# Attention's output projection of a batch: in one group through the pair banks, or in eight one-bank pieces through the score ring, over six groups

## The reference, cut to what matters

```
q, k = rope(x @ Wq.T + bq), rope(x @ Wk.T + bk)        # 16 heads, two maps (1, 2) of 16 columns each
s1, s2 = q1 @ k1.T / 4, q2 @ k2.T / 4                  # 1024 x 1024, causal
attn = softmax(s1) - lam * softmax(s2)
out = attn @ v                                         # per head 1024 x 16
out = out * rsqrt(mean(out * out, -1) + eps) * head_norm_w * (1 - li)
x = layernorm(x + out.reshape(B, S, 256) @ Wo.T + bo)
```

## Time and profile before

| | us |
|---|---|
| median of 3 runs | 2443.26 |
| lowest, highest | 2440.05, 2448.67 |
| the profiled execution | 2444.31 |
| its span (first to last instruction) | 2442.5 |
| mean granted TensorE clock in it | 0.966 of full |
| PE busy in the span | 2217.5 (91%) |
| DVE, ACT, POOL busy | 1581.1, 1244.2, 713.6 |
| the 32 groups, between ACT's copies at step 6 of groups 1 and 31 | 1358.14 to 2220.72 |

### The profile page before, as it was taken

One profiled execution on the slowest core, in us unless ns is written; L12 is line 12 of the kernel. 1 busy time (PEld: TensorE's weight loads), 2 busy tenths in 40 slices (PEclk: granted clock), 3 DMA queues, 4 the chain that ended last, 5 costly groups with the idle time before them and its releaser, 6 DMA issues.

```text
span 2442.5 us, 50583 instructions
## 1 busy us (share of the span) xinstructions
PE 2217.5 (91%) x17816; PEld 1367.4 (56%) x17816; DVE 1581.1 (65%) x2653; ACT 1244.2 (51%) x2537; POOL 713.6 (29%) x797
## 2 busy tenths in 40 slices
PE   7999999889999999976866999899989998999998
PEld 5777777556666666655652333333333334347887
DVE  3556666643333333338999888788878887844878
ACT  6666665213433322323322778777767876774110
POOL 1222322102333333325553232422232342223000
PEclk9999999999999999988885999999999999999999
DMA  4223334651222222232431011010001100210000
GB/s 170 87 87 103 114 113 164 207 200 32 53 36 38 38 36 38 38 98 97 164 141 41 28 48 39 30 43 33 32 25 52 37 28 28 63 37 1 18 26 27
DMA packets 89900, 164.19 MB, mean 67 GB/s; under 512 B 15952, under 2 KB 64080, under 8 KB 88000
## 3 DMA queue, kind: packets, MB, share of 16 engines
q1 hardware_dynamic: 76032, 142.20, 16.9%
q0 software_dynamic: 13632, 18.77, 4.8%
HBM read 99.91 MB, written 60.49 MB: 66 GB/s over the span
## 4 chain that ended last, share of the span: by engine, by line
PE 54%; DVE 11%; ACT 6%; issue 5%; DMA 2%; SPq 0%; POOL 0%; ACTq 0%; DVEq 0%
PE PS L2169 10%; PE PS L1404 8%; PE PS L58 6%; PE PS L60 6%; PE PS L59 6%; PE PS L2232 6%; PE PS L2193 4%; ACT E L1983 4%; DVE NM L2079 3%; PE PS L2188 2%; PE PS L1389 2%; DVE X L2416 2%; DVE TT L1597 2%; PE PS L2123 1%; PE PS L2144 1%
## 5 line engine op out<-in xcount | busy, mean ns | idle before, releaser
L2079 DVE TENSOR_REDUCE NM<-PS 128x2 f32<-128x1024 f32 (+3 forms) x608 | 679.9, 1160 | 138.2 <-PE PS L2193 131.9
L1983 ACT ACTIVATE E<-PS 128x512 f32<-128x512 f32 (+2 forms) x1280 | 626.1, 560 | 206.7 <-PE PS L2232 194.9
L2169 PE MATMUL PS<-E,VP 128*32 128x256 f32 (+1 forms) x5120 | 370.8, 371 | 0.5 <-ACT OT L2010 0.5
L1916 POOL TENSOR_SCALAR_AFFINE_SELECT E<-E 128x512 f32<-128x512 f32 x256 | 162.5, 635 | 411.7 <-ACT E L1983 411.6
L1201 DVE SCALAR_TENSOR_TENSOR XIL<-PS,XSC,XIH 128x128 f16<-128x128 f32 x142 | 43.2, 346 | 335.4 <-ACT XIH L997 335.4
L2232 PE MATMUL PS<-QK 50*128 50x512 f16 (+3 forms) x1152 | 214.2, 329 | 16.2 <-ACT E L1983 16.0
L1032 ACT ACTIVATE HB<-PS 128x768 f32<-128x768 f32 x71 | 57.6, 811 | 300.8 <-PE PS L1389 300.8
L2169 PEld LDWEIGHTS PS<-E,VP 128*32 128x32 f32 x5120 | 108.4, 109 | 161.0 <-issue 117.3
L1404 PE MATMUL PS<-WALL,HB 128*128 x852 | 195.7, 379 | 1.0 <-ACT HB L1032 1.0
L2193 PE MATMUL PS<-QK 48*128 48x512 f16 (+3 forms) x1152 | 180.6, 344 | 9.6 <-DVE NM L2079 9.0
L941 POOL DMA_INDIRECT XB<-x_normed,IDX x71 | 71.1, 1001 | 364.9 <-DVE GAT L1217 315.5
(11 more groups left out here) (347 smaller groups left out, 4178.6 us busy)
## 6 DMA issues: line engine op xcount, KB each, us to landing
parts<-PP SPq DMA_DIRECT2D x32, 512.0 KB, 3.0
WIN<-in_we SPq DMA_DIRECT2D x16, 768.0 KB, 5.2
QK<-parts SPq DMA_DIRECT2D x96, 128.0 KB
WALL<-pairs_of_weights SPq DMA_DIRECT2D x7, 1536.0 KB
pairs_of_weights<-WPH SPq DMA_DIRECT2D x16, 384.0 KB, 2.3
pairs_of_weights<-WPL SPq DMA_DIRECT2D x16, 384.0 KB, 3.2
WALL<-in_we SPq DMA_DIRECT2D x8, 768.0 KB
QK<-parts SPq DMA_DIRECT2D x96, 64.0 KB
```

The costliest lines, as they stand in the source:

```text
L1916: e.affine_select(out=E[:, m % NE, :, 0:128], in_=E[:, m % NE, :, 0:128], pattern=[[0, 4], [1, 128]], compare_op=ALU.is_ge, fill=0.0, base ...
L1983: e.activation(dst, src, ACT.Exp, scale=unit).then_inc(S.ex, 1)
L2079: e.tensor_reduce(dst, src, AX, ALU.max).then_inc(S.mx, 1)
L2169: a = e.matmul(PS[32 * jj:32 * jj + 32, 7, 512 - n + c0:512 - n + c1], VP[b % 2][:, kt, 17 * hd:17 * hd + 32], E[:, m % NE, jj, c0:c1], st ...
```

## The change

The loops over steps are replaced by one generator `steps()`, which yields for every step the letters of a table (s scores, v products, m maximum, x select, and so on), and after the last letter of a step the mark "end". It leaves scores, products and maxima in the order of before. On POOL, one mask of E (step 5) goes ahead of the two small copies of the row maxima, in each group. The end of a batch is then laid out anew by tables with keys (group of the batch, step):

- DVE's sum of squares is four instructions of 512 values, at the ends of steps 16, 18, 20, 22 of group 8b + 8 (`meant`).
- POOL scales one eighth a step in steps 2 to 9 of group 8b + 9 (`scaled`).
- the transposes are four pieces of four (`joined`), at the ends of steps 12 and 18 of groups 8b + 9 and 8b + 10, each into one bank and copied out by one ACT instruction of 128x512.
- the product with Wo is four pieces of four matmuls (`put_out`), at the end of step 12 of groups 8b + 11 to 8b + 14, each into one bank; DVE adds 128x512 at the end of step 13 (`added`) and takes two moments; roots at step 15 (`rooted`) and norms at 17 and 19 (`normed`) of groups 8b + 12 and 8b + 14.
- these eight pieces take their turns in the ring of the three score banks (`single`), and no longer in the pair banks. The score tile that comes third after a piece takes the bank of that piece: it waits for ACT's copy (`S.pj`) or DVE's add (`S.op`) in place of an exponential.

The diff, cut:

```diff
+    STEPS = (
+        "msvm", "svxm", "svm", "sxO", "srRm", "svxhLm", "svH", "svxm", "svm", "svm", "svm", "sodm", "sAm",
...
+    halves = [(0, 0), (0, 1), (1, 0), (1, 1), (2, 0), (3, 0)] + [(4 + k // 2, k % 2) for k in range(12)] + [(10, 0), (11, 0)]
+    OVER = 3
...
+    joined = {(1, 12): 0, (1, 18): 1, (2, 12): 2, (2, 18): 3}
+    put_out = {(3, 12): 0, (4, 12): 1, (5, 12): 2, (6, 12): 3}
+    added = {(3, 13): 0, (4, 13): 1, (5, 13): 2, (6, 13): 3}
+    rooted = {(4, 15): 0, (6, 15): 1}
+    normed = {(4, 17): 0, (4, 19): 1, (6, 17): 2, (6, 19): 3}
+    squared = {(0, 13 + i): i for i in range(8)}
+    scaled = {(1, 2 + i): i for i in range(8)}
+    all_squared = (0, 23)
+    meant = {(0, 16): 0, (0, 18): 1, (0, 20): 2, (0, 22): 3}
...
+    def single(key, sem, value):
+        bank = singles[len(single_turns) % 3]
+        single_turns[key] = (bank, single_freed.get(bank))
+        single_freed[bank] = (sem, value)
...
+        if c == "s" and w >= 0:
+            for i in scores_of(w, s):
+                single(("score", i), S.ex, i + 1)
+        if c == "end":
+            if k in joined:
+                single(("join", b, joined[k]), S.pj, 4 * b + joined[k] + 1)
+            if k in put_out:
+                single(("out", b, put_out[k]), S.op, 4 * b + put_out[k] + 1)
...
+        def join_part(b, j):
+            kb, _ = single_turns["join", b, j]
+            c = slice(512 * (j // 2), 512 * (j // 2) + 512)
+            e.wait_ge(S.pe_pj, 4 * b + j + 1)
+            e.wait_ge(S.ms, 4 * b + 4)
+            e.activation(OTT[:, j % 2, c], PS[:, kb, :], ACT.Copy).then_inc(S.pj, 1)
...
-    def norm_x(e, b, q):
-        xs = [X[:, 8 * b + 4 * q + i, :] for i in range(4)]
-        e.wait_ge(S.rs4, 2 * b + q + 1)
-        layernorm_apply(e, K, xs, xs)[-1].then_inc(S.xd, 1)
...
+        def means_of(b, c):
+            e.wait_ge(S.sq1, 8 * b + 2 * c + 2)
+            e.tensor_reduce(MS[:, 32 * c:32 * c + 32], OB[:, 2 * c:2 * c + 2, :].rearrange("p i (h d) -> p (i h) d", d=16), AX, ALU.add).then_inc(S.ms, 1)
+
+        def add_out(b, q):
+            kb, _ = single_turns["out", b, q]
+            xs = X[:, 8 * b + 2 * q:8 * b + 2 * q + 2, :]
+            e.wait_ge(S.pe_op, 4 * b + q + 1)
+            e.wait_ge(S.bo, b + 1)
+            e.tensor_tensor(xs, xs, PS[:, kb, :].rearrange("p (i d) -> p i d", i=2), ALU.add).then_inc(S.op, 1)
+
+        def moments(b, q):
+            c, t0 = 2 * (q % 2), 8 * b + 2 * q
+            e.wait_ge(S.op, 4 * b + q + 1)
+            a = layernorm_stats(e, own.dve, K.ST[:, c:c + 2, :], K.MV[:, c:c + 2, :], [X[:, t0 + i, :] for i in HALF])
+            if q % 2:
+                a.then_inc(S.mv4, 1)
+
+        def norm_two(b, q):
+            e.wait_ge(S.rs4, 2 * b + q // 2 + 1)
+            for i in HALF:
+                x, c = X[:, 8 * b + 2 * q + i, :], 2 * (q % 2) + i
+                a = e.tensor_scalar(x, x, K.MV[:, c, 0:1], K.RS[:, c:c + 1], ALU.subtract, ALU.mult)
+            if q % 2:
+                a.then_inc(S.xd, 1)
...
+                if k in meant:
+                    means_of(b, meant[k])
+                if k in normed:
+                    norm_two(b, normed[k])
+                if k in added:
+                    add_out(b, added[k])
+                    moments(b, added[k])
...
+        def join_part(b, j):
+            kb, free = single_turns["join", b, j]
+            k, h = j % 2, j // 2
+            e.wait_ge(*free)
+            e.wait_ge(S.osc1, 8 * b + 4 * h + 4)
+            for i in QUAD:
+                a = e.transpose(PS[:, kb, 128 * i:128 * i + 128], OA[b % 2][:, 4 * h + i, 128 * k:128 * k + 128], K.IDN[:])
+            a.then_inc(S.pe_pj, 1)
+
+        def out_part(b, q):
+            kb, free = single_turns["out", b, q]
+            e.wait_ge(*free)
+            e.wait_ge(S.pj, 4 * b + 2 * (q // 2) + 2)
+            e.wait_ge(S.hnw, 2)
+            for i in HALF:
+                t = 2 * q + i
+                for k in HALF:
+                    a = e.matmul(PS[:, kb, 256 * i:256 * i + 256], OTT[:, k, 128 * t:128 * t + 128], WO1[:, k, :], start=k == 0, stop=k == 1)
+            a.then_inc(S.pe_op, 1)
...
+                    kb, free = single_turns["score", i]
+                    if free:
+                        e.wait_ge(*free)
```

More of the change, by code:

```diff
@@ L1907, in pool @@
         low_rows(1)
[L1908 to L1925, removed]
+        for w, s, c, k in steps():
+            if c == "L" and 1 <= w < 31:
+                low_rows(w + 1)
+            if c == "x" and w >= 0:
+                m = 12 * w + diagonal[k]
+                e.wait_ge(S.ex, exps_to(m + 1))
+                e.affine_select(out=E[:, m % NE, :, 0:128], in_=E[:, m % NE, :, 0:128], pattern=[[0, 4], [1, 128]],
+                                compare_op=ALU.is_ge, fill=0.0, base=0, channel_multiplier=-1).then_inc(S.sel, 1)
+            if c == "A" and w >= 1:
+                add_heads(w - 1)
+            if c == "end" and k in squared:
+                square(w // 8 - 1, squared[k])
+            if c == "end" and k in scaled:
+                scale(w // 8 - 1, scaled[k])
         add_heads(31)
@@ L1963, in act @@
         unit = e.alloc_register("score_unit")
         e.reg_load(unit, K.SCL[0:1, 0:1].bitcast(I32))
[L1966 to L2000, removed]
-                put_rows(w + 2)
-            if w == -2:
-                lambdas()
@@ new lines, in act @@
+        for w, s, c, k in steps():
+            if c == "s" and w >= 0:
+                exponentials(w, s)
+            if c == "o" and w >= 0:
+                out_of(e, w, 0)
+            if c == "O" and w >= 1:
+                out_of(e, w - 1, 1)
+            if c == "H" and w >= 1:
+                take_heads(e, w - 1)
+            if c == "R" and 1 <= w < 31:
+                put_rows(w + 1)
+            if w < 0 and c == "m" and k == NU - 1:
+                put_rows(w + 2)
+                if w == -2:
+                    lambdas()
+            if c == "end":
+                b = w // 8 - 1
+                if k == all_squared:
+                    roots(e, b)
+                if k in joined:
+                    join_part(b, joined[k])
+                if k in rooted:
+                    root4(e, b, rooted[k])
@@ new lines, in norm_two @@
+        def norm_two(b, q):
[5 more added lines that the diff above has]
+                a.then_inc(S.xd, 1)
+        for w, s, c, k in steps():
+            if c == "m" and w + 2 < 32:
+                maximum(w + 2, k)
+                if k == NU - 1:
+                    combine(w + 2)
+                    if w == -2:
+                        differences()
+                    if w == -1:
+                        factors()
+            if c == "d" and w >= 1:
+                denominators(e, w - 1)
+            if c == "end":
+                b = w // 8 - 1
@@ new lines, in next_half @@
+        def next_half(n):
+            j, half = halves[n % 20]
+            products(12 * (n // 20) + j, half)
+        for w, s, c, k in steps():
+            if c == "m" and w + 2 < 32:
+                maximum(w + 2, k)
+                if w < 0 and k == NU - 1:
+                    put_rows(w + 2)
+            if c == "s" and w >= 0:
+                scores(w, s)
+            if c == "v" and 20 * w + k >= OVER:
+                next_half(20 * w + k - OVER)
+            if c == "r" and 1 <= w < 31:
+                put_rows(w + 1)
+            if c == "h" and w >= 1:
+                pe_heads(e, w - 1)
+            if c == "end":
+                b = w // 8 - 1
```

240 lines of the change are left out of this document (111 added, 129 removed).

## The result

| us | before | changed |
|---|---|---|
| median | 2446.68 (7 runs, 2440.05 to 2453.46) | 2466.93 (7 runs, 2460.48 to 2471.55) |
| profiled execution | 2444.31 | 2469.59 |

The change makes the kernel slower: the ratio is 1.0082, with a 95% interval of 1.0061 to 1.0102. I forecast 2453 with a range from 2440 to 2463. The direction was right; the size was not, and 2466.93 lies above the range.

The account below looks back on a forecast made before the run. PE, busy 91% of the span, was taken as the bound. The profiled 2444.3 us + 3.5 for pieces, transposes and group 8 + 5.6 for the clock gave 2453.4, forecast as 2453, range 2440 to 2463.

Parts of the forecast that it names:

- the stop: PE at step 14's first score tile after an output piece waits 1.9 us for DVE's add, queued behind a reduction.
- The sum: Without the clock: 14.7 per batch in place of 13.39, group 8 1.85 in place of 1.99; three batches +3.5 us.
- the transposes: Four pieces a batch at steps 12 and 18, PE or ACT paid each time: 0.5 us each, 2.0 per batch.
- group 8: PE held at the second pair of score tiles, by ACT instead of DVE: +1.85 us in place of +1.99.
- the clock: Falls to 1.2 GHz at 0.63 us a stop, 15 stops: 9.4 us in place of 3.75, +5.6.
- rival 2: The clock falls after nearly every stop: 2460.3 us, or 2464 at 1.34 us a fall; chance 0.14.
- My one in three: Share of PE's stops followed by a clock fall, from two falls after six stops in the kernel before.
- "slower": The whole kernel measures above 2450.6 us, beyond the 0.3% that can be told from no change; chance 0.56.
- Rival 3: Step 14 does not stop in groups with pieces: 1.9 us a piece, 22.8 in all, total 2423; chance 0.10.

Follow-up runs that it names:

- the half-filled run: The changed kernel with two extra matmuls of unused result on PE in the stop, in 11 of 12 groups with pieces: 2458.69 us, ratio 1.0041.
- the moved add: The changed kernel with DVE's add of an output piece ahead of the reduction of step 13's unit: 2432.93 us, ratio 0.9953.
- unequal distances: The changed kernel with the first and third output piece of a batch at step 16, their adds at step 17: 2464.6 us, ratio 1.0069.
- the whole sum: The changed kernel with the sum of squares in one DVE instruction at its place of before: 2465.24 us, ratio 1.0083.
- the run with the pair banks: The changed kernel with the four output pieces of a batch in turns of the pair banks, not the score banks: 2463.17 us, ratio 1.0077.

## Why the prediction was right and wrong

**Right: the place and the cause of the stop.** The sum had 1.9 us of stop, from a reduction of 0.95 and an add of 0.69. It counted from 0.24 after the start of the unit of step 13; counted so, the stop measured is 1639.23 - 1637.42 = 1.81 (the profile's 1.65 counts from the unit's end). The piece's own matmuls take 1.92 to the next tile, not 1.83, and these two errors cancel. What is left over is small: a piece costs 3.24 and 3.53 us without the clock, forecast 3.03 and, in the groups with roots, 3.38. Over the 12 pieces that is 39.6 us against the 12.0 + 0.7 a batch of the sum, 38.1.

**Wrong in size: the transposes.** "0.5 each, 2.0 per batch", by the half of a pair on PE or on ACT. Measured 1.40 a group, 2.8 per batch, inside the bounds I gave; 2.4 us in all. Moved to step 22 they took 0.19 less a piece; that this is ACT's copy, uncovered at step 18, is not shown, and the busy times above speak rather for PE.

**Right: group 8.** Forecast 1.85 above an ordinary group, measured 1.84, and by ACT. That PE's stop there comes from ACT's root, waiting for the last quarter, is in the rows, and the stop went when root and quarters were moved away.

**Wrong: the clock.** This is the step that failed: "The cost was 3.75 / 6 = 0.63 a stop", taken from two falls after six stops, and from there 5.6 us. The three stops in groups 8, 16 and 24 had no fall in this profile, but of the 12 new stops all 12 were followed by one. The groups with pieces hold 17.0 us above their lengths without falls (29.40 and 29.69, and 27.85 for group 29, from the half-filled run; for group 30 the 34.49 of the moved add and the 1.91 by which its group 12 is shorter), and group 31 0.8: 17.8 less the 3.75 of before is 14.0 against 5.6. The 14 falls so cost 1.27 each on average; it is above all the share that the term had wrong. It is rival 2 that came about, whose +12.5 is near the 14.0. Among stops at the end of group 8, 16 or 24 the share is about a half: 13 falls after 24 of them, in the eight profiles that have them (before, changed, and six experiments); where the stop was taken away, 0 of 9. My one in three was two falls in six, too few to lean on. The six left out a third stop a batch of the kernel before, of 1.29, 1.29 and 1.20 us, none of them with a fall; with it the share would have been two in nine, further still from what came. The one in group 9:

```profile
1601.25 0.23 PE L2188 MATMUL PS<-MR 64*128 64x64 bf16 x4 [1.29 <-DVE NM L2079]
```

And I gave the case in which all fall 14 chances in 100 without asking what differs between one stop and twelve alike.

**What stays open** is why 12 of 12. A group with a fall lasts 30.7 us, so the next stop comes 30.72 us after the last, and the falls too: four in a row in each batch. With unequal distances 7 of 12 fell, with the same distances and a whole sum 9 of 12. That the equal distance keeps the falls going was argued and fits, but one profile each doesn't show it. Where the series broke off, the fall had moved against the stop: with the whole sum it begins 0.34, 0.18 and 0.03 us after the stop's end in groups 11, 12 and 13, and group 14 has none, while in the changed kernel it stays at 1.45 to 1.50 through the same four groups. That the falls in the groups with pieces come from the stop is shown: filling it, wholly or by half, left none of 22 groups with a fall, and moving the add none of 12. It isn't shown that every fall needs one: the two others of the changed kernel's profile had none before them.

The sum by parts, against the profiled difference: without the clock -0.5 for group 8 and its like, -31.7 for groups 9 and 10 and theirs, +39.6 for the pieces, +7.4 (forecast +3.5), clock +14.0 (+5.6), the part up to group 1 +3.8 (nothing forecast, and nothing of the change): 25.2 of 25.28 us. The medians are 20.2 apart.

Of the chances: "slower" had 0.56 and came true. Rival 3's price was sound: with the add moved the 12 groups take 336.8 us in place of 376.7; 22.9 of that is the stops, against its 22.8, and 17.0 the falls. Of these 39.8 us 4.3 are lost again to falls in groups 16 and 24; the medians are 34 apart.

## What to carry to other kernels

When a small tenant enters a ring of banks, look at what its reader is queued behind: the wait appears at the tenant that comes one round later, and its length is the reader's queue, not the reader. Spreading a block of work gains only what the block waited; each new place has to be read for its own wait. And price a stop of the busiest engine with its clock, from the profile: once with the share of falls that was seen and once with a fall at every stop, and if the second changes the verdict, take the stop away before trusting a share from six cases.

## What the runs showed of the hardware

PE standing still 1.65 us once in a group of about 30 us was followed by a fall to 1.2 GHz in 12 of 12 groups of the changed kernel, in 9 of 12 with the whole sum and in 7 of 12 with unequal distances (with 2.10 us in group 30 each time). A stop of 0.94 us was met by one in 4 of 11 groups, one of 0.6 us in none of 11. One fall of 3.41 us cost 1.0 to 1.3 us in the changed kernel; in the run with the pair banks, where the piece's matmuls ran at the lower clock, up to 1.7 (31.13 us against 29.44). In the run with the whole sum, groups of the same work took 29.7 us without and 30.9 with it. Useless matmuls in the place of waiting made the kernel 11 us faster.
